# A GpSimd no-op and a wait on its end behind every dispatch scatter of a two-layer mixture-of-experts kernel

## What is computed

```
# layer 0: one of 16 experts for each token
h = x @ cond_w[subject] + cond_b[subject]            # 128 x 128 weights by row of the batch
scores = sigmoid(logits) * onehot(argmax(logits)),   logits = h @ router.T
expert = (up * silu(gate)) @ down[e],  gate, up = split((score * h) @ gate_up[e])
x = x + shared(h) + expert

# layer 1: two of 8 experts for each token, each expert with 1280 places
h = layernorm(x + adapter[language](x)) * gamma[language] + beta[language]
idx1, idx2 = best and second expert; pos1, pos2 = place of the token in its expert
                                                     # (second choices stand behind all first ones)
y[token] = sum over k of gate_k * (silu(h @ w1[e_k] + b1) @ w2[e_k] + b2)   # dropped if pos >= 1280
x = x + y + 0.1 * (silu(h @ sw1 + sb1) @ sw2 + sb2)
```

## Time and profile before

| what | us |
|---|---|
| median of 3 runs | 514.65 (514.14 to 516.04) |
| span of the profiled execution | 571.1 |
| TensorE busy in it | 463.1 (81%) |
| VectorE / ScalarE / GpSimd busy | 261.9 / 255.9 / 238.0 |
| dispatch scatters, layer 0 (L571): 32, busy | 32.6 |
| dispatch scatters, layer 1 (L605): 64, busy | 63.6 |

### The profile page before, as it was taken

How to read it: one execution, slowest core, us unless ns; L and a number is a source line. 1 busy time by engine, 2 the same in 40 slices (tenths; PEclk the granted TensorE clock), 3 DMA queues, 4 the chain that set the end, 5 groups by cost and what they waited for, 6 DMA issues and landing times.

```text
span 571.1 us, 10130 instructions
## 1 busy us (share of the span) xinstructions
PE 463.1 (81%) x3132; PEld 392.7 (69%) x3133; DVE 261.9 (46%) x831; ACT 255.9 (45%) x596; POOL 238.0 (42%) x255
## 2 busy tenths in 40 slices
PE   6897698978888889999846765489999999999910
PEld 3785564566676766787744655178999999999900
DVE  1144267845555554347447912053433333233475
ACT  2453453235555543556314241034455555555653
POOL 2023535214554555003272777600155555556550
PEclk8997879999999999999787796579999999999975
DMA  9999921102222107400010111110223434313569
GB/s 242 365 340 368 367 66 37 39 23 67 74 71 63 47 11 235 143 2 20 19 51 15 48 48 55 42 47 1 61 76 96 134 107 113 105 50 88 165 182 282
DMA packets 70930, 62.33 MB, mean 109 GB/s; under 512 B 9676, under 2 KB 57439, under 8 KB 70898
## 3 DMA queue, kind: packets, MB, share of 16 engines
q1 hardware_dynamic: 63202, 48.32, 28.5%
q0 software_dynamic: 7168, 12.56, 6.7%
q10 hardware_dynamic: 528, 1.05, 0.6%
HBM read 32.44 MB, written 31.69 MB: 112 GB/s over the span
## 4 chain that ended last, share of the span: by engine, by line
PE 63%; another core or an unknown queue 10%; DVE 9%; DMA 7%; issue 6%; ACT 2%; POOL 1%; SPq 0%; DVEq 0%; POOLq 0%; ACTq 0%
PE PS L1645 11%; PE PS L1304 8%; PE PS L1361 6%; PE PS L1603 5%; PE PS L1441 3%; PE PS L1635 3%; PE PS L1565 3%; PE PS L1633 3%; PE PS L1634 3%; PE PS L1393 2%; PE PS L1402 2%; DMA back1b<-grp_y,grp_i 2%; PE PS L1426 2%; PE PS L1428 1%
## 5 line engine op out<-in xcount | busy, mean ns | idle before, releaser
L623 POOL DMA_INDIRECT back<-grp_y,grp_i x70 | 69.8, 997 | 93.9 <-DVE grp_y L1236 71.0
L605 POOL DMA_INDIRECT rows<-disp,slot x64 | 63.6, 994 | 76.1 <-DVE slot L1072 56.0
L1645 PE MATMUL PS<-w2r,act 128*128 128x128 f32 x640 | 78.1, 275 | 0.5 <-ACT act L789 0.5
L1645 PEld LDWEIGHTS PS<-w2r,act 128*128 128x128 f32 x640 | 74.8, 192 | 0.9 <-DVE grp_y L1236 0.7
L582 POOL DMA_INDIRECT back<-act,blk_i x48 | 46.9, 977 | 60.8 <-DVE act L1015 41.1
L789 ACT ACTIVATE act<-PS,b1r 128x256 f32<-128x256 f32 x160 | 63.7, 477 | 16.5 <-PE PS L1635 14.2
L571 POOL DMA_INDIRECT rows<-disp,slot x32 | 32.6, 1018 | 67.4 <-issue 53.8
L1236 DVE TENSOR_TENSOR grp_y<-PS,b2r 128x256 f32<-128x256 f32 x40 | 17.0, 424 | 89.6 <-PE PS L1645 69.5
L1603 PE MATMUL PS<-sw,act 128*128 128x128 f32 x256 | 37.5, 313 | 14.1 <-issue 11.8
L1633 PE MATMUL PS<-xh,w1h 128*128 128x256 f32 x160 | 48.3, 302 | 0.0
L740 ACT ACTIVATE act<-PS,sb 128x512 f32<-128x512 f32 x32 | 21.4, 688 | 59.6 <-remote 32.9
(11 more groups left out here) (256 smaller groups left out, 1009.9 us busy)
## 6 DMA issues: line engine op xcount, KB each, us to landing
rows<-zrow SPq DMA_DIRECT2D x32, 260.0 KB, 5.0
grp_x<-rows SPq DMA_DIRECT2D x40, 130.0 KB
w_raw<-in_f_gate_up SPq DMA_DIRECT2D x8, 512.0 KB, 10.1
back<-zrow SPq DMA_DIRECT2D x8, 512.0 KB
back<-back SPq DMA_DIRECT2D x16, 256.0 KB, 5.0
blk_x<-rows SPq DMA_DIRECT2D x48, 65.0 KB
acc<-in_x SPq DMA_DIRECT2D x8, 256.0 KB, 5.8
y0g<-back SPq DMA_DIRECT2D x8, 256.0 KB, 3.2
```

The source lines that it names most:

```text
L605: gp.indirect_dma_start(rows1, bass.IndirectOffsetOnAxis(ap=slot[:, k, t:t + 1], axis=0), disp[:, t, :], None, bounds_check=E1 * CAP - 1, ...
L623: gp.indirect_dma_start(back, bass.IndirectOffsetOnAxis(ap=grp_i[v % NX][:, u:u + 1], axis=0), grp_y[k][:, u, :], None, bounds_check=last, ...
L1645: last = mm(PS[5 + k][:, u * P:(u + 1) * P], act[k][:, c, u * P:(u + 1) * P], w2r[e][:, c, :], start=c == 0, stop=c == C1 - 1)
```

## The change

Behind each of the 96 dispatch scatters an empty GpSimd instruction is put, which adds 1 to a new semaphore `sent` at its end. GpSimd's sequencer then waits until `sent` has reached the number of scatters so far.

```diff
+        sent = sem("sent")
...
             for t in range(NT):
...
                 gp.indirect_dma_start(rows0, bass.IndirectOffsetOnAxis(ap=slot[:, 0, t:t + 1], axis=0),
                                       disp[:, t, :], None, bounds_check=NBLKP * P - 1,
                                       oob_is_err=False).then_inc(sc0[t // G % 2], 16)
+                gp.engine_nop().then_inc(sent, 1)
+                pool.wait_ge(sent, t + 1)
...
                     gp.indirect_dma_start(rows1, bass.IndirectOffsetOnAxis(ap=slot[:, k, t:t + 1], axis=0),
                                           disp[:, t, :], None, bounds_check=E1 * CAP - 1,
                                           oob_is_err=False).then_inc(sc1[k][t // HT], 16)
+                    gp.engine_nop().then_inc(sent, 1)
+                    pool.wait_ge(sent, NT + k * NT + t + 1)
                     if (k, t) in ((0, NT - 8), (1, HT - 8)):
```

## The result

| kernel | median us | runs |
|---|---|---|
| before | 514.76 | 514.14 to 516.04 |
| changed | 546.61 | 545.58 to 548.71 |

The changed kernel is 31.9 us slower; the ratio is 1.061, with a 95% interval of 1.056 to 1.066. The forecast was 549.0 us (520 to 575).

What follows compares the result with a forecast made beforehand. Layer 1's dispatch scatters were taken to set when the grouped experts start, within a mostly TensorE chain. Layer 0's 0, layer 1's 32.7 and TensorE's restart 1.7 gave +34.4 us on 514.65: 549 us, range 520 to 575.

Steps and rivals of the forecast that it cites:

- The stalls: Waits beside dispatch scatters in the first profile, 15.2, 10.0 and 26.4 us, claimed to be absent from the timed runs.
- the clean schedule: The first profile's 571.1 us span less the stalls of 15.2, 10.0 and 26.4 us: 519.5 us.
- The first rival: Stalls beside dispatch scatters are real, come from far-ahead issue, and the change removes them: 17.2 us less, 497.5 us; chance 0.12.
- The period: Start-to-start time of dispatch scatters on GpSimd: 1.95 us after the change, 0.67 more than the 1.28 before.
- The lower end, 1.78: Scatter period in us if the empty instruction takes nothing, 0.97 + 0.81; forecast time then 540 us.
- Layer 1: 64 scatters whose last end moves from 359.1 to 391.8, delaying the grouped experts with nothing to cover it: +32.7 us.
- P: The start-to-start period of dispatch scatters on GpSimd: 1.28 us before, forecast 1.95 after, range 1.78 to 2.28.
- TensorE's restart: TensorE's first 32 matmuls after standing still some 39 us take 5.45 us instead of 3.73: +1.7 us.
- Layer 0 is covered: 32 scatters hidden by layer 0's shared experts, block landed at 103.5 and wanted at 104.4: 0 us.
- P = 2.28: Upper scatter period in us, empty instruction after 0.30 and taking 0.20; layer 0 then loses 9.4 us, time 579 us.
- rival 2: The wait doesn't hold the sequencer to the scatter's end; period stays 1.28 us, time 514 to 516 us; chance 0.08.
- rival 3: Cheap handover: issue overlaps the scatter's tail, period some 1.5 us (1.28 plus a bare semaphore's 0.2), 523 us; chance 0.13.

## Why the prediction was right, step by step

1. **The stalls have no place in the timed runs.** Right: the sum of the clean schedule, 519.5 us, is within 5 us of the 514.8 of the undisturbed profile. But I laid them on profiling, and the second profile has none. What caused them in that one execution stays open. The first rival, a gain of 17 us, fell with it: no run shows stalls to be gained back. The rule that the forecast took from the Trainium skill, Runtime: NRT & Kernel Launch, section The ~15µs preamble/postamble breakdown, a profile's total some 6.2 us longer than the reported time, is not seen here: in the repeated run the reported time is the longer one, 516.97 us against a span of 514.8, 2.2 us apart. The 50 us that this rule would have left to the timed runs are in none of them.
2. **The period.** Forecast 1.95 us, measured 1.81. The mis-sized term is the empty instruction: 0.07 + 0.1 us were taken from L612's start and a guess for an instruction without data; it starts at the scatter's very end and takes 0.04, and a second pair of it and its wait costs 0.07. The lower end, 1.78, was the better guess. The rest, 0.8 us from release to start, was right to the row.
3. **Layer 1.** Forecast +32.7 us, measured 121.7 - 91.5 = +30.2 (from 248.25 to 369.96 after; 249.06 to 340.59 before). Errors cancel in part, which is luck. With P = 1.81 my working gives 384.1 - 359.1 = +25.0, 7.7 less than forecast. Against that, my baseline was 2.3 us too long (93.8 against 91.5), and the dispatch after is 2.9 us longer than the 118.8 of that working: single scatters took longer (mean 1.020 us against 0.993 in the repeated profile), and the second scatter of the second choices starts 1.59 us behind the one in front instead of 0.83. That one has no gate; the same 1.59 stands at the same scatter in the runs with the wait in layer 1 only and on the second choices only, and its cause was not found. That the scatters bound the place before the change, that the rounds absorb part of the first choices and that everything of the second counts, was each shown by a run.
4. **TensorE's restart.** Forecast +1.7 us; in these two profiles it is 4.91 - 5.74 = -0.8. The 32 matmuls behind the wait take 4.91 us after; in the kernel before they take 5.74 and not 3.73, since TensorE already stands still for 6.61 us there (with 8 scatters fewer, and no wait, they take 3.81). The rows are windows (busy times of the engines, then the granted clock, DMA share, GB/s): the 7 us around the matmuls and the stretch at their start, first of the changed kernel, then of the kernel before:

```profile
373.00:380.00 7.00, 6.31 (x44) 6.34 (x45) 1.46 (x4) 0.77 (x2) 0.00 (x0) 0.74 0.50 134
373.60:376.00 2.40, 2.31 (x11) 2.34 (x12) 0.57 (x2) 0.38 (x1) 0.00 (x0) 0.50 0.78 189
```

```profile
343.00:350.00 7.00, 5.76 (x32) 5.79 (x33) 0.59 (x2) 0.38 (x1) 0.00 (x0) 0.58 0.57 151
344.20:347.00 2.80, 2.76 (x13) 2.79 (x14) 0.52 (x2) 0.38 (x1) 0.00 (x0) 0.50 0.79 194
```

   Both resume at 0.50, the lower of the two levels (1.2 and 2.4 GHz), and the 0.74 and 0.58 over 7 us are mixes, since the clock rises sooner in the changed kernel. The length of the wait doesn't order the restart: with the wait on the first choices (19.29 us) the same matmuls take 6.32 us, on the second (22.85 us) 4.95. So the term is worth between nothing and a gain or loss of about 1 us, and its sign is not shown. The step compared with the undisturbed matmuls instead of with those in the same place of the clean schedule.
5. **Layer 0 is covered.** Right: 1.005 (0.999 to 1.011) with one wait and 1.000 (0.997 to 1.003) with two. But the spare was mis-sized. Forecast was 1 us (103.5 against 104.4); by tile, the loads and transposes of the blocks (first and last start) in the changed kernel and the transposes in the repeated profile of before are

```profile
L451 SPq DMA_DIRECT2D blk_x<-rows x48: 328/333/473, 100.9 to 184.7; - x48
L1309 PE MATMUL PS<-ident,blk_x x48: 271/273/329, 110.3 to 187.5; 128*128 128x128 f32 x48
```

```profile
L1304 PE MATMUL PS<-ident,blk_x x48: 270/273/328, 109.8 to 188.4; 128*128 128x128 f32 x48
```

   With 1.8 us to land, a block loaded at 100.9 is there some 7 us before it is wanted. Taking all of 15.2 us off 119.56 put the clean transpose at 104.4, where the undisturbed kernel has it at 109.8. So the forecast of 0 us didn't hang on 1 us, and the 9.4 us of loss at P = 2.28 would have been about 4.
6. **Rivals 2 and 3.** The wait does hold the sequencer to the scatter's end, and nothing of the start overlaps with its tail. With one scatter of lead the distance is rival 2's 1.28 us. The 0.2 us of a bare semaphore in rival 3 stands in no row of the forecast; a second empty instruction with its wait measured 0.07.

The sum, 0 + 32.7 + 1.7 = 34.4 us, is 2.5 over the 31.9 measured. The two profiles lie 28.9 us apart (543.7 - 514.8) and layer 1 alone gives 30.0 on its own chip, so an agreement within 3 us is as much as these numbers can tell.

## What to carry to other kernels

A sequencer that waits for the end of what it has just issued lays bare the issue of the next one, here 0.53 us more for each scatter, of which the empty instruction and the wait are some 0.07. If a queue has to be throttled, try a wait for the one before: here one in flight hid all of it. Before pricing an added wait, ask which chain it is in and what its slack is; 32 scatters with slack cost nothing that could be measured, and 64 with little or none cost 30 us.

And compare a profile's span with the timed median before reading it. Where they differ by 50 us, price the change on the schedule without the odd stalls, or profile again.

## What the runs showed that was not expected

- One profiled execution of the kernel before was 56 us longer than the others, with VectorE, ScalarE and TensorE held up beside the scatters; a second one of the same kernel took 516.97 us. The cause was not found.
- A scatter from a released sequencer starts 0.75 to 0.8 us after the release, while an empty instruction behind a scatter, its end and a wait for it together take 0.07 us.
- The second scatter of the second choices starts 1.59 us behind the first in every profile with the wait on it (0.83 elsewhere), with no releaser in the trace.
- The sequencer made its move for the last scatter of layer 1 when twelve others were still to start, (368.15 - 352.4) / 1.28. With an empty instruction behind each scatter and no wait the lead is 336.16 - 328.2 = 8.0 us, six scatters with their six empty instructions, so again about twelve instructions. The Trainium skill, Advanced Engine Details and Errata, section Engine Queue Depths, gives GpSimd a queue of 8; the lead in these traces is longer. No run depends on it, since a lead of one was enough.
